# An attention stage rebuilt: most key tiles turned by DMA, low halves on GpSimd, queries made in stage one

## The reference

```python
keys = jnp.einsum('nj,hjk->hnk', node_matrix, Wks)
queries = jnp.einsum('nj,hjk->hnk', node_matrix, Wqs)
values = jnp.einsum('nj,hjk->hnk', node_matrix, Wvs)
atts = jnp.einsum('hqk,hmk->hqm', queries, keys) / key_dim ** 0.5
atts = atts - 1e+16 * (1.0 - adj)[None, :, :]
atts = jax.nn.softmax(atts, axis=-1)
return jnp.einsum('hqm,hmk,hko->qo', atts, values, Wo)
...
x = _layernorm(x + _L0_gnn_ref(x, adj, L0_gnn_Wks, L0_gnn_Wqs, L0_gnn_Wvs, L0_gnn_Wo), axis=-1)
```

## Time and profile before

| | us |
|---|---|
| median of 3 runs | 2949.29 (2943.21 to 2949.56) |
| the profiled execution, its own time | 2943.13 |
| its span in the trace | 2941.3 |
| stage one | 0 to 143 |
| attention | 143 to 1624 |
| edge attention | about 2090 to 2630 |

### The profile page before, as it was taken

How to read it: one execution, slowest core, us unless ns; L and a number is a source line. 1 busy time by engine, 2 the same in 40 slices (tenths; PEclk the granted TensorE clock), 3 DMA queues, 4 the chain that set the end, 5 groups by cost and what they waited for, 6 DMA issues and landing times. The chain is left out here.

```text
span 2941.3 us, 64010 instructions
## 1 busy us (share of the span) xinstructions
PE 2752.5 (94%) x23308; PEld 1788.8 (61%) x23308; DVE 1862.5 (63%) x3387; ACT 1553.4 (53%) x2376; POOL 392.8 (13%) x372
## 2 busy tenths in 40 slices
PE   8989999989989998989899799979899999979998
PEld 6667676767767776767676444457444444434443
DVE  4479897988879798988897322245444555633222
ACT  4467786867768687767687222222343334324222
POOL 0001111111111111111111012300111111210222
PEclk9999999999999999999999899989999999989999
DMA  4221111111111111111110345531455667743454
GB/s 157 81 80 39 39 38 39 38 39 51 48 53 39 39 38 39 38 39 39 44 48 5 129 145 203 198 110 46 115 140 148 185 177 190 201 116 113 172 209 145
DMA packets 220379, 280.58 MB, mean 95 GB/s; under 512 B 138721, under 2 KB 157153, under 8 KB 208865
## 3 DMA queue, kind: packets, MB, share of 16 engines
q1 hardware_dynamic: 220128, 277.13, 30.3%
HBM read 195.39 MB, written 38.44 MB: 79 GB/s over the span
## 5 line engine op out<-in xcount | busy, mean ns | idle before, releaser
L760 DVE SCALAR_TENSOR_TENSOR att_pt_low<-att_ps_t,att_pt_high 128x512 f16<-128x512 f32 (+1 forms) x1056 | 633.5, 641 | 102.0 <-ACT att_pt_high L729 85.8
L729 ACT ACTIVATE att_pt_high<-att_ps_t 128x512 f16<-128x512 f32 (+1 forms) x1056 | 538.6, 559 | 288.6 <-PE att_ps_t L661 286.7
L661 PE MATMUL att_ps_t<-all_ident,att_scores 128*128 128x128 f32 (+1 forms) x3872 | 539.5, 280 | 73.8 <-issue 67.5
L767 DVE CUSTOM_DVE_ANT_0 att_scores<-att_slots,att_adj 128x1024 f32<-128x1024 f32 x528 | 574.2, 1088 | 12.0 <-PE att_slots L673 11.5
L735 ACT ACTIVATE att_scores<-att_scores,att_nmax 128x1024 f32<-128x1024 f32 x528 | 553.8, 1049 | 11.0 <-DVE att_nmax L773 11.0
L673 PE MATMUL att_slots<-l_kk,att_q 128*128 128x512 f16 x2112 | 498.4, 359 | 7.0 <-DMA att_q<-att_q_raw 5.6
L661 PEld LDWEIGHTS att_ps_t<-all_ident,att_scores 128*128 128x128 f32 (+1 forms) x3872 | 410.2, 139 | 110.8 <-issue 74.6
L1276 PE MATMUL a_ps<-l_y,a_adj 128*128 128x512 f16 (+1 forms) x1936 | 431.2, 382 | 9.0 <-DVE a_adj L1290 4.7
L643 PE MATMUL att_ps_pv<-l_vv,att_pt_high 128*128 128x129 f16 (+1 forms) x3872 | 433.6, 221 | 0.4 <-DVE att_pt_low L760 0.4
L643 PE MATMUL att_ps_pv<-l_vv,att_pt_low 128*128 128x65 f16 (+1 forms) x3872 | 403.6, 193 | 0.0
L643 PEld LDWEIGHTS att_ps_pv<-l_vv,att_pt_high 128*128 128x128 f16 (+1 forms) x3872 | 351.6, 98 | 63.5 <-issue 2.5
(11 more groups left out here) (140 smaller groups left out, 2938.9 us busy)
## 6 DMA issues: line engine op xcount, KB each, us to landing
l_adj<-in_adj_cols SPq DMA_DIRECT2D x44, 1408.0 KB, 6.1
att_adj<-in_adj SPq DMA_DIRECT2D x22, 1354.0 KB, 6.0
l_adj_tiles<-in_adj SPq DMA_DIRECT2D x22, 1354.0 KB, 5.9
p_x_in<-x SPq DMA_DIRECT2D x66, 256.0 KB, 2.6
att_q<-att_q_raw SPq DMA_DIRECT2D x88, 128.0 KB, 2.3
a_xres<-x SPq DMA_DIRECT2D x44, 256.0 KB, 2.7
scores_rows<-edge_raw SPq DMA_DIRECT2D x8, 842.0 KB, 3.4
p_x_in<-in_x SPq DMA_DIRECT2D x22, 256.0 KB, 2.6
```

Of the source, the lines that this page charges most:

```text
L661: mm = nc.tensor.transpose(ps_t[0:r, g % 2, (k % GB) * P:(k % GB + 1) * P], sp_sb[:, h % 2, k * P:k * P + r], ident[:, :])
L729: nc.scalar.activation(pt[0][:, g, 0:w], ps_t[:, g % 2, 0:w], ACT.Copy, scale=P_S) \
L760: nc.vector.scalar_tensor_tensor(out=pt[1][:, g, 0:w], in0=ps_t[:, g % 2, 0:w], scalar=P_S, in1=pt[0][:, g, 0:w], op0=ALU.mult, op1=ALU.su ...
L767: nc.vector.tensor_tensor_reduce(out=sp_sb[:, h % 2, lo:lo + width], in0=slots[:, (NC * h + c) % 2, 0:width], in1=adj[:, u, lo:lo + width] ...
```

## The change

Stage one gets a third product: the queries are made there, 48 more matmuls for each of the 22 tiles, and their halves are stored in row layout (`q_rows`); `xt` is no longer stored. The attention stage loads them with four DMAs a tile, and its once-a-tile query product, the two splits after it and the spread are gone.

In the attention stage the row of scores is cut into pieces of 1024, 768 and 916 columns (`PIECES`). The first two, 14 key tiles, are split into halves in row layout and turned by DMA (`part` to `far`); only the last 8 key tiles are turned by the matmul engine (`near`), in two groups with a bank each. The high half of piece 0 is made by ScalarE; the low half of piece 0, and both halves of piece 1, by GpSimd. The factor 1024 that keeps the low halves in range is now an addition of its logarithm to the negated largest (`largest`). The product with the values is three matmuls of 65, 64 and 65 columns for each key tile in place of two of 129 and 65, and all three add into the same 65 columns, so that GpSimd has nothing left to add. A unit now stretches over five steps in place of four (scores, exponential, turning, products, copy out). The loop covers 18 tiles in 9 turns (20 tiles in 10 turns before).

```diff
--- before.py
+++ after.py
+PIECES = [(0, 1024), (1024, 768), (1792, N - 1792)]
+TURNED = 2
+TK = PIECES[TURNED][0] // P
+TURN_GROUPS = [list(range(TK, TK + GB)), list(range(TK + GB, T))]
+NT = len(TURN_GROUPS)
...
+            def loads(m, u):
+                t = 2 * m + u
+                if not is_tile(m, u, T) and not is_tile(m, u, T - 1):
                     m1, u1 = after(m, u)
+                    if not is_tile(m, u, 0):
+                        sp.wait_ge(slot_free, PER_TILE * t)
...
-                if not last:
-                    spread(m, u)
+                    load_q(t + 1, u1)
                 if not is_tile(m, u, 0):
...
+            def step(m, u, h, on):
+                if h == 1:
+                    loads(m, u)
+                if on(1):
+                    i, _t, _u, h1, same = unit(m, u, h, 1)
+                    v = h1 % 2
+                    for c in range(TURNED):
+                        lo, width = PIECES[c]
+                        k = slice(lo // P, (lo + width) // P)
+                        if not early(i, 2):
+                            wait_apart(sp, far_used[c], i - 1, pad_clear)
+                        for a, made in enumerate((part_high[c], part_low[c])):
+                            wait_apart(sp, made, i + 1, pad_clear)
+                            sp.dma_start_transpose(far[a][:, v, k, :], part[a][:, v, lo:lo + width]) \
+                                .then_inc(far_ready[c][v], 16)
...
+            def low(i, v, c):
+                lo, width = PIECES[c]
+                wait_apart(pool, part_high[c], i + 1, pad_clear)
+                nc.gpsimd.tensor_tensor(out=part[1][:, v, lo:lo + width], in0=sc[:, v, lo:lo + width],
+                                        in1=part[0][:, v, lo:lo + width], op=ALU.subtract).then_inc(part_low[c], 1)
+
+            def step(m, u, h, on):
+                if on(1):
+                    i, _t, _u, h1, same = unit(m, u, h, 1)
+                    v = h1 % 2
+                    low(i, v, 0)
+                    lo, width = PIECES[1]
+                    if not early(i, 2):
+                        wait_apart(pool, far_ready[1][v], 32 * same, pad_clear)
+                    wait_apart(pool, exp_done, NC * i + 2, pad_clear)
+                    nc.gpsimd.tensor_copy(part[0][:, v, lo:lo + width], sc[:, v, lo:lo + width]) \
+                        .then_inc(part_high[1], 1)
+                    low(i, v, 1)
...
+                if h == 5 and not is_tile(m, u, T - 1) and not is_tile(m, u, T):
...
+                if h == 7 and not is_tile(m, u, 0):
...
+                if g == 0:
+                    pe.wait_ge(exp_done, NC * (i + 1))
+                if not early(i, 1):
+                    pe.wait_ge(near_low, NT * (i - 1) + g + 1)
+                for n, k in enumerate(TURN_GROUPS[g]):
                     r = rows_of(k)
...
+                    mm = nc.tensor.transpose(ps_t[0:r, g, n * P:(n + 1) * P], sc[:, v, k * P:k * P + r], ident[:, :])
+                mm.then_inc(turned, 1)
+
+            def products(v, h, keys):
+                for k in keys:
+                    r = rows_of(k)
+                    halves, n = (far, k) if k < TK else (near, k - TK)
+                    for a, b in ((0, 0), (0, 1), (1, 0)):
+                        cols = slice(KD, P + 1) if b == 0 else slice(0, KD)
+                        mm = nc.tensor.matmul(ps_pv[:, 0:cols.stop - cols.start], halves[a][0:r, v, n, :],
+                                              vv[0:r, k, h, cols], start=k == TK and a + b == 0,
+                                              stop=k == TK - 1 and a == 1)
...
+            def near_products(i, v, h):
+                if not early(i, 1):
+                    pe.wait_ge(pv_out, i)
+                pe.wait_ge(near_low, NT * (i + 1))
+                products(v, h, range(TK, T)).then_inc(near_used, 1)
+
+            def far_products(v, h, same, c):
+                lo, width = PIECES[c]
+                pe.wait_ge(far_ready[c][v], 32 * same + 32)
+                products(v, h, range(lo // P, (lo + width) // P)).then_inc(far_used[c], 1)
...
+                if on(0):
+                    if h == 0:
+                        pe.wait_ge(q_loaded[u], 64 * (m + 1))
+                    scores(i, u, h, 0)
+                    scores(i, u, h, 1)
+                if on(2):
+                    j, _t, _u, h2, _same = unit(m, u, h, 2)
+                    turn(j, h2 % 2, 0)
+                    turn(j, h2 % 2, 1)
+                if on(3):
+                    j, _t, _u, h3, same = unit(m, u, h, 3)
+                    near_products(j, h3 % 2, h3)
+                if on(0):
+                    scores(i, u, h, 2)
+                if h == 7 and not is_tile(m, u, 0):
+                    pe.wait_ge(misc_free, 2 * t - 1)
+                    product3(nc, ps_misc[:, 0:D], lambda a, j: ot[:, a, j, :], lambda b, j: wo[b][:, j, :]) \
+                        .then_inc(misc_full, 1)
+                if on(3):
+                    far_products(h3 % 2, h3, same, 0)
+                    far_products(h3 % 2, h3, same, 1)
...
+            def step(m, u, h, on):
+                if on(4):
+                    i, _t, ou, h4, _same = unit(m, u, h, 4)
+                    act.wait_ge(far_used[1], i + 1)
+                    nc.scalar.activation(pv[:, ou, h4, :], ps_pv[:, 0:KD + 1], ACT.Copy).then_inc(pv_out, 1)
+                if on(1):
+                    i, _t, _u, h1, same = unit(m, u, h, 1)
+                    v = h1 % 2
+                    exp(i, v, 0)
+                    lo, width = PIECES[0]
+                    if not early(i, 2):
+                        act.wait_ge(far_ready[0][v], 32 * same)
+                    act.wait_ge(exp_done, NC * i + 1)
+                    nc.scalar.activation(part[0][:, v, lo:lo + width], sc[:, v, lo:lo + width], ACT.Copy) \
+                        .then_inc(part_high[0], 1)
+                    exp(i, v, 1)
+                    exp(i, v, 2)
+                if on(2):
+                    i, _t, _u, h2, _same = unit(m, u, h, 2)
+                    if not early(i, 2):
+                        act.wait_ge(near_used, i - 1)
+                    for g, tiles in enumerate(TURN_GROUPS):
+                        w, n = P * len(tiles), tiles[0] - TK
+                        act.wait_ge(turned, NT * i + g + 1)
+                        nc.scalar.activation(near[0][:, h2 % 2, n:n + len(tiles), :],
+                                             ps_t[:, g, 0:w].rearrange("p (k r) -> p k r", r=P), ACT.Copy) \
+                            .then_inc(near_high, 1)
...
+            def mask(i, u, h, c):
+                v, (lo, width) = h % 2, PIECES[c]
+                if not early(i, 2):
+                    if c == TURNED:
+                        dve.wait_ge(turned, NT * (i - 1))
+                    else:
+                        dve.wait_ge(part_low[c], i - 1)
+                wait_apart(dve, slot_full, NC * i + c + 1, pad_clear)
...
+                if on(0):
+                    mask(i, u, h, 1)
+                    mask(i, u, h, 2)
+                    largest(i, h % 2)
+                if on(2):
+                    j, _t, _u, h2, _same = unit(m, u, h, 2)
+                    for g, tiles in enumerate(TURN_GROUPS):
+                        w, n = P * len(tiles), tiles[0] - TK
+                        dve.wait_ge(near_high, NT * j + g + 1)
+                        nc.vector.tensor_tensor(out=near[1][:, h2 % 2, n:n + len(tiles), :],
+                                                in0=ps_t[:, g, 0:w].rearrange("p (k r) -> p k r", r=P),
+                                                in1=near[0][:, h2 % 2, n:n + len(tiles), :], op=ALU.subtract) \
+                            .then_inc(near_low, 1)
...
+                def queries(_t, u, bank):
+                    return [(bank.rearrange("p (c r) -> p c r", c=J), q_halves[:, u, 0, :, :], q_halves[:, u, 1, :, :],
+                             Q_S / 8.0 * XW)]
+
+                project(nc, s, "p0", x, ident, [(wk, *key), (wv, *value), (wq, *query)],
+                        [("cols", *key, keys), ("rows", *value, values), ("cols", *query, queries)],
+                        kept=(2, q_halves, q_rows), later=[(wo, *output)],
...
```

425 lines of the change are left out of this document (163 added, 262 removed).

## The result

| | before | after |
|---|---|---|
| median, us | 2946.55 (2943.21 to 2949.56, 4 runs) | 2813.70 (2807.18 to 2815.72, 4 runs) |
| ratio | | 0.9548, interval 0.9537 to 0.956 |
| stage one | 0 to 143 | 0 to 206 |
| attention | 1481 | 1294 |

The account below looks back on a forecast made before the run. VectorE was taken to set the pace, 7.04 us a unit of attention, with the matmul engine 5% behind. From 2943.1 us, attention -234 and stage one +62 gave 2771, stated as 2772; range 2650 to 2895.

Parts of the forecast that it names:

- Stage one, +62: Stage one: 48 key matmuls take 2.68 us a tile, 59 for 22 tiles, plus 3 us for more weights.
- Start, 10 us: Start of the attention stage: 10 us in place of 15, with no query product before the first scores.
- The engines, 5.4 to 6.0: Attention units: six resources would each need 5.4 to 6.0 us a unit, GpSimd the most at 6.0.
- The DMA engines, 5.8 a unit: Attention units: 917 KB of turned halves take 4.8 us at 192 GB/s, the loads about 1.
- The collision, 3.5 us a tile: Attention units: turning DMAs queue behind next-tile loads, 8.4 us late once a tile; 3.5 show, 0.4 a unit.
- Turns of the loop, 9 times 9: Attention loop: 9 turns at 9 us each, 81 us, with each wait in the body staying.
- The clock: Matmul engine in the attention stage: a granted clock below 0.95 would show the forecast wrong.
- The sum: Whole kernel: units at 6.4 us, 176 of them 1126; attention 1247 in place of 1481; 2771 in all.
- slow turning DMAs: Rival, SyncE's queue: at 1.94 us an instruction a unit takes 8.2 us, 3088 in all; decides from 1.7; chance 0.10.
- GpSimd slower than in proportion: Rival, GpSimd's low halves: at 3.1 ns a column the pace is 7.0 us and the time 2877; chance 0.08.
- The clock rival: Rival, matmul engine: the lower clock level, 0.50, in half of the units gives 3190 us; chance 0.07.
- All hidden (0.15): Rival, attention units: cheaper GpSimd low halves and slack hiding the adjacency load; pace 5.7 us, 2650 in all; chance 0.15.

Follow-up runs that it names:

- e11: e10 with only the high halves turned, one DMA of 14 tiles a unit: 2625.85 us, 0.8926 of the kernel before.
- e10: The changed kernel with two turning DMAs a unit, next-tile loads spread over the steps and the largest value in two operations: 2748.70 us, 0.9335 of the kernel before.
- e4: The changed kernel with GpSimd making low halves of only the first 128 columns of each piece: 2818.13 us, 0.957 of the kernel before.

## Why the prediction was right or wrong

- **Stage one, +62:** 63 (143 to 206).
- **Start, 10 us:** 14. Counted as in the earlier trace rows, to the first mask operation, it is 206 to 220.3 (row below); the window above, to 225, takes in the first unit. `diagonal` waits 8.8 us for the adjacency rows, which are asked for at 210.8 us, behind the last store of the queries in stage one and the first query loads. I had counted that load from the start of the stage, and not what the new store puts ahead of it.

```profile
220.28 1.23 DVE L766 CUSTOM_DVE_ANT_0 att_scores<-att_slots,att_adj 128x1024 f32<-128x1024 f32 x1 [2.69 <-POOL att_adj L597]
```

- **The engines, 5.4 to 6.0:** too high. A calm unit takes 5.37 us with all of them in it (64 of the 175 distances are 5.5 or less), and with half of the transfers away (e11) the median is 5.39. VectorE, ScalarE and GpSimd are busy 5.1, 5.1 and 5.2 us a unit, once-a-tile work included. GpSimd's operations are below proportion, as the groups of the changed kernel by shape show (busy, mean ns; 2.1 ns a column where the earlier trace rows gave 2.56), so GpSimd is 74% busy where I said 85:

```profile
L603 POOL TENSOR_TENSOR att_part_low<-att_scores,att_part_high 128x1024 f16<-128x1024 f32 x171 | 365.4, 2137 | 261.8 <-ACT att_part_high L735 261.5
L603 POOL TENSOR_TENSOR att_part_low<-att_scores,att_part_high 128x768 f16<-128x768 f32 x170 | 280.6, 1650 | 24.7
```

- **The DMA engines, 5.8 a unit:** the term of the sum that was mis-sized. It is 1214/176 = 6.9: 6.0 for the turned halves where I had 4.8, since they move at 153 GB/s here and not at the 192 of the one window of 1 us in the earlier trace rows, and 0.9 for the loads, where I had 1. By this term alone the pace would be 6.9, 176 x 0.5 = 88 us over my 6.4.
- **The collision, 3.5 us a tile:** in the tile shown it is a wait of 7.0 us of ScalarE and a gap of 8.7, over 20 tiles 7.9 in the mean: nearly all of the 8.4 late. The step that failed is "the last half is wanted in the fourth step, about T + 3S - 1": that is when the matmul engine reads it. ScalarE wants the same transfer done earlier, before it may write `part` again, right behind the exponential of two units later, T + 2S + 1.2. The low half of piece 0 is the second DMA of its unit and lands 3.6 us after issue (median), at T + S + 1.3 + 3.6. By that the slack is S - 3.7, 1.7 us at the calm pace of 5.37 where I had 4.5 to 5, and 8.4 - 1.7 = 6.7 is close to the 7.0 of the tile shown. The row that I named as its sign, the wait of the matmul engine for `far`, is there at 115 to 129 us, but ScalarE's 168 is ahead of it.
- **Turns of the loop, 9 times 9:** 8.1 at each of the 8 seams between 9 turns, 65 and not 81. **The tail, 30:** 36 from the last mask operation, as counted in the earlier trace rows.
- **The clock:** 0.93 in the units, under the 0.95 that I gave as a sign of error. It follows the waits: behind the block of the timeline above, matmuls of 65 columns take 0.24 us in place of 0.19; in e10, without blocks, it is 0.98. How much of a block's 7.9 us is this clock and not the wait itself is not parted.
- **The sum:** +4 at the start, 1244 in place of 1207 for units and turns (+37), +6 at the end, +1 in stage one: 48 us over 2771, or 2819. The profiled execution took 2815.72, since the layers behind attention were 3 us shorter in it. The pace without the turns is (1244 - 65)/176 = 6.7, so 6.4 was near, but partly by luck: calm units were half a us or more faster than the 6.0 I took for the engines, and the DMA term and the collision were both too small. The sign and the range rested on the gain over 7.04 being larger than either.
- **The rivals:** slow turning DMAs did not come at 1.7 us an instruction (1.23 and 1.28 in the median), but as bytes, a milder form. GpSimd slower than in proportion is refuted by its rows (2.1 ns a column) and by e4. The clock rival wanted the low level in half of the units; 0.93 is a mild form of it, whose price is not measured. All hidden (0.15) would have had no collision, and it shows.

## What to carry to other kernels

Slack of a transfer ends at its first waiter, and that may be the engine that wants the source buffer back, not the one that reads the result. For each shared resource work out two numbers, its total work and how late it makes the chain in one bad place; when they come out within some per cent of each other, as here, an experiment that takes one away can show nothing, and only both together show either. Read a stage by the distances of all its units and not by one: the mean of 7.05 us was hardly ever the time of a unit. A part of a change that looks like a cost (63 us of products moved to an earlier stage) can pay by itself, if the work that it removes stood in the chain.

## What was unexpected of the hardware

An operation of three columns took up to 1.65 us, 452 ns on average, and in the timeline above ended when GpSimd's running operation did (at 936.88 and 936.87 us); as two operations of one SBUF input each it took 156 and 154 ns, and with short GpSimd operations 162 (these three are medians). The Trainium skill (GPSIMD Engine Reference, Specifications) says that GpSimd's SBUF interfaces are shared with VectorE, and that VectorE's instructions with two SBUF inputs contend. The trace agrees, and in it the wait is that of the whole running operation.

Joining four turning DMAs to two, with the same bytes, took 57 us of transfers off 1214, 0.16 us for each of 352 instructions less; splitting the adjacency loads in three and spreading the loads added 48. Both are differences of shares with two decimals, good to some 10 us; the lines of queue 1 have 72 and 29 for the same two steps.
